# The opening of a fused attention and mixture-of-experts kernel rearranged: who rounds the weights and the context, where the second context half lands, and when batch 0 makes its values

## The reference

```python
x = x + tanh(g_xattn) * attention(layernorm(x), ctx, Wq, Wk, Wv, Wo, bo)   # 8 batches, 512 queries, 1024 keys, 8 heads of 64
x = x + tanh(g_ffn)   * moe(layernorm(x), router, w_pre, w_gate, w_post)   # 8 experts, top 2, capacity, 4096 tokens
```

## Time and profile before

| | us |
|---|---|
| median of 3 runs | 1797.45 |
| lowest, highest | 1796.33, 1798.6 |
| the profiled execution's own time | 1798.76 |
| its span | 1796.9 |

### The profile page before, as it was taken

One profiled execution on the slowest core, in us unless ns is written; L12 is line 12 of the kernel. 1 busy time (PEld: TensorE's weight loads), 2 busy tenths in 40 slices (PEclk: granted clock), 3 DMA queues, 4 the chain that ended last, 5 costly groups with the idle time before them and its releaser, 6 DMA issues. The chain is left out here.

```text
span 1796.9 us, 35848 instructions
## 1 busy us (share of the span) xinstructions
PE 1681.8 (94%) x13198; PEld 1532.6 (85%) x13199; DVE 1270.6 (71%) x2667; ACT 1053.7 (59%) x2229; POOL 678.2 (38%) x619
## 2 busy tenths in 40 slices
PE   5799999999999999999999986599999999999997
PEld 4688888888888888888888875499999999999997
DVE  5688888888888888888988886555555555545443
ACT  3666766666766767667766764244454454545443
POOL 4243344444444444444344323232333333333323
PEclk9999999999999999999999997699999999999999
DMA  6100001010010010010000021432323233231211
GB/s 192 36 10 15 24 25 36 25 36 25 25 36 25 25 36 25 25 36 25 25 25 25 24 71 55 155 101 35 100 37 92 54 75 100 29 104 25 36 30 24
DMA packets 65117, 85.55 MB, mean 48 GB/s; under 512 B 7208, under 2 KB 53800, under 8 KB 65008
## 3 DMA queue, kind: packets, MB, share of 16 engines
q1 hardware_dynamic: 47680, 64.08, 11.3%
q0 software_dynamic: 15984, 18.82, 6.0%
q10 hardware_dynamic: 1344, 1.20, 0.2%
HBM read 54.59 MB, written 29.48 MB: 47 GB/s over the span
## 5 line engine op out<-in xcount | busy, mean ns | idle before, releaser
L699 POOL TENSOR_SCALAR probs<-probs,row_rec 128x1024 f32<-128x1024 f32 x256 | 284.5, 1123 | 490.6 <-DVE row_rec L1525 477.7
L1064 ACT ACTIVATE pt_h<-turned 128x512 fp32r<-128x512 f32 x512 | 279.9, 602 | 218.1 <-PE turned L839 218.0
L1240 DVE TENSOR_TENSOR pt_l<-turned,pt_h 128x512 fp32r<-128x512 f32 x512 | 331.2, 680 | 7.0 <-ACT pt_h L1064 6.0
L1456 DVE TENSOR_REDUCE neg_max<-scores 128x1 f32<-128x1024 f32 x256 | 301.2, 1217 | 38.5 <-PE scores L827 38.5
L839 PE MATMUL turned<-ident,probs 128*128 128x128 f32 x2048 | 282.7, 280 | 30.2 <-DVE pt_l L1240 20.1
L839 PEld LDWEIGHTS turned<-ident,probs 128*128 128x128 f32 x2048 | 224.4, 142 | 98.1 <-issue 66.8
L1113 ACT ACTIVATE probs<-scores,neg_max 128x1024 f32<-128x1024 f32 x256 | 285.2, 1117 | 4.4 <-DVE neg_max L1456 4.3
L943 PE MATMUL ring<-pt_h,v_hl 128*128 128x256 f32 x1024 | 263.7, 295 | 5.5 <-DVE v_hl L1240 5.3
L1692 DVE TENSOR_TENSOR act_f<-ffn,silu 128x256 f32<-128x256 f32 x288 | 122.1, 424 | 195.6 <-ACT silu L1194 190.3
L943 PE MATMUL ring<-pt_l,v_hl 128*128 128x256 f32 x1024 | 253.0, 285 | 0.0
L1194 ACT ACTIVATE silu<-ffn 128x256 f32<-128x256 f32 x288 | 110.6, 384 | 227.4 <-PE ffn L804 216.9
(11 more groups left out here) (221 smaller groups left out, 4060.8 us busy)
## 6 DMA issues: line engine op xcount, KB each, us to landing
w_raw<-w_t SPq DMA_DIRECT2D x16, 1024.0 KB
e_rows<-lists SPq DMA_DIRECT2D x37, 260.0 KB, 2.7
ctx_raw<-ctx_t SPq DMA_DIRECT2D x16, 512.0 KB, 3.8
wg_raw<-wg_t SPq DMA_DIRECT2D x8, 1024.0 KB
lists<-rows SPq DMA_DIRECT2D x8, 520.0 KB, 8.2
x_in<-x SPq DMA_DIRECT2D x8, 512.0 KB, 3.9
x_sum<-x SPq DMA_DIRECT2D x8, 512.0 KB, 3.9
out<-x_sum SPq DMA_DIRECT2D x8, 512.0 KB, 2.9
```

The source lines that it names most:

```text
L699: nc.gpsimd.tensor_scalar(probs[:, k, :], probs[:, k, :], row_rec[:, k:k + 1], 1.0, ALU.mult, ALU.mult).then_inc(scaled, 1)
L1064: return nc.scalar.activation(dst, src, ACT.Copy)
L1240: return nc.vector.tensor_tensor(dst, src, hi_part.bitcast(F32), ALU.subtract)
L1456: nc.vector.tensor_reduce(neg_max[:, k:k + 1], scores[:, n % 2, :].rearrange("p (a c) -> p a c", a=2), AX.XY, ALU.max, negate=True).then_i ...
```

## The change

It touches only what runs before step 9 of batch 0:

- START becomes five jobs in a list of their own, `START_JOBS`: x, x, k, q, k. The four value jobs of batch 0 go into FIRST: two in step 0, one in step 1, one in step 2 (`FIRST_VALUES`).
- ACT rounds the first context half, wk and wq in the order in which they are loaded, then the second context half, and wv after the first k job. Its tanh moves to step 4 of FIRST, behind that step's exponential, and DVE's product of bias and tanh to step 7.
- The second context half is loaded into `probs[:, 2, :]`, right behind wq and without a wait; wk is loaded before wq. The 8 padding writes follow the loads with no wait for the context in front of them.
- DVE makes the lo part of the first context half, between two pieces of the layer norm, and normalises x. POOL keeps the power and makes the lo part of the second context half.
- PE no longer waits for the small inputs at its start, but before step 8 of FIRST.

```diff
+START_JOBS = [("x", 0, 0), ("x", 1, 0), ("k", 0, 0), ("q", 0, 0), ("k", 0, 1)]
+FIRST_VALUES = {0: [("v", 0, 0), ("v", 0, 1)], 1: [("v", 0, 2)], 2: [("v", 0, 3)]}
...
             def start():                                  # SP
                 load_x(0, x_in, x_loaded)
-                load_ctx(0, 0)
-                for i, (w, dst) in enumerate(((wq, probs[:, 0, :]), (wk, probs[:, 1, :]),
...
+                load_first_ctx(0)
+                load_first_raw(0)
+                load_first_raw(1)
+                load_first_ctx(1)
+                load_first_raw(2)
...
-                sp.wait_ge(ctx_split, 1)
-                load_ctx(0, 1)
...
+            power(0, 0)                                   # POOL
+            pool.wait_ge(ctx_hi, 2)
+            nc.gpsimd.tensor_tensor(ctx_l[:, :, M // 2:M], first_ctx_raw(1),
+                                    ctx_h[:, :, M // 2:M].bitcast(F32), ALU.subtract)\
+                .then_inc(ctx_split, 1)
...
-            pe.wait_ge(small_loaded, 64)                  # PE
+            for [(what, c)] in START.steps:
+                run_job(START, NEXT_FROM, what, c)
...
-            act.wait_ge(small_loaded, 64)                 # ACT
-            nc.scalar.activation(tanh_g[:, :], tanh_g[:, :], ACT.Tanh).then_inc(tanh_done, 1)
+                split_first_ctx(0)
+                split_raw(0)
+                split_raw(1)
+                drain(START, NEXT_FROM, *x0)
+                drain(START, NEXT_FROM, *x1)
+                split_first_ctx(1)
+                drain(START, NEXT_FROM, *k0)
+                split_raw(2)
+                drain(START, NEXT_FROM, *q0)
+                drain(START, NEXT_FROM, *k1)
...
+                for part in range(4):                     # DVE
+                    layer(0, 0, x_in, part)
+                v.wait_ge(ctx_hi, 1)
+                lo(ctx_l[:, :, 0:M // 2], ctx_raw[:, :, :], ctx_h[:, :, 0:M // 2])\
+                    .then_inc(ctx_split, 1)
+                for part in range(4, 8):
+                    layer(0, 0, x_in, part)
+                v.wait_ge(ln_ready[0], 1)
+                for q in range(QT):
+                    nc.vector.tensor_scalar(x_in[:, q, :], x_in[:, q, :], norm[:, 0, 4, q:q + 1],
+                                            norm[:, 0, 5, q:q + 1], ALU.mult, ALU.add)\
+                        .then_inc(normed[0], 1)
+                split_first(0)
+                split_first(1)
+                drain(START, NEXT_FROM, *x0)
+                drain(START, NEXT_FROM, *x1)
+                drain(START, NEXT_FROM, *k0)
+                split_first(2)
+                drain(START, NEXT_FROM, *q0)
+                drain(START, NEXT_FROM, *k1)
```

More of the change, by code:

```diff
@@ L113, in __init__ @@
         self.steps, place = [], offset
-        for u in range(UNITS if own or nxt else END_STEPS):
+        for u in range(UNITS if own else END_STEPS if prev else len(START_JOBS)):
             mine = []
+            if not own and not prev:
+                self.steps.append([(START_JOBS[u], place)])
+                place += 1
+                continue
+            if not prev:
+                mine += FIRST_VALUES.get(u, [])
             if u % 4 in (1, 2) and (prev if u < 5 else own):
@@ L130, in __init__ @@
         self.where = {job: c for step in self.steps for job, c in step}
+        self.early = {job: c for step in self.steps[:NEXT_FROM] for job, c in step
+                      if not prev and own and job[:2] == ("v", 0)}
     def results(self, u):
@@ L135, in results @@
             return self.steps[u - 1]
-        return [(job, c - RING) for job, c in self.before.steps[-1]] if self.before else []
+        return [(job, c - RING) for job, c in self.before.steps[-1]] if self.prev else []
     def of(self, b):
@@ L142, in place @@
     def place(self, job):
+        if job in self.early:
+            return self.early[job]
         if SLOT_OF[job] < NEXT_FROM:
@@ L388, in wait_all_drained, with first_raw, whole, first_ctx_raw @@
                     wait_drained(eng, body, max(of_bank))
+        def first_raw(i):
+            flat = x_sum[:, :, :].rearrange("p q d -> p (q d)")
+            return ((wk, wk_h, wk_l, probs[:, 0, :]), (wq, wq_h, wq_l, probs[:, 1, :]),
+                    (wv, wv_h, wv_l, flat))[i]
+        def whole(t):
+            return t[:, :, :].rearrange("p c n -> p (c n)")
+        def first_ctx_raw(half):
+            if half == 0:
+                return ctx_raw[:, :, :]
+            return probs[:, 2, :].rearrange("p (c m) -> p c m", c=KC)
         def batches(eng, run):
-            run(START)
             run(FIRST)
@@ L527, in run @@
                         load_w(sp, i, 0)
+            start()
             batches(sp, run)
@@ L947, in do_job, with run_job @@
                 last.then_inc(filled, 1)
+            def run_job(body, u, what, c):
+                reads = wait_for_job(body, u, what)
+                wait_all_drained(pe, body, reads + [c - 2])
+                do_job(what, ring[:, c % 2, :])
             def run(body):
                 for u, jobs in enumerate(body.steps):
+                    if body is FIRST and u == 8:
+                        pe.wait_ge(small_loaded, 64)
                     if body.own and u % 2 == 0:
@@ L1064, in hi, with split_raw, split_first_ctx @@
                 return nc.scalar.activation(dst, src, ACT.Copy)
[L1066 to L1069 removed]
+            def split_raw(i):
+                _, dst, _, raw = first_raw(i)
+                act.wait_ge(raw_loaded[i], 16)
+                hi(whole(dst), raw).then_inc(raw_hi, 1)
+            def split_first_ctx(half):
+                act.wait_ge(first_ctx[half], 16)
+                hi(ctx_h[:, :, half * (M // 2):(half + 1) * (M // 2)], first_ctx_raw(half))\
+                    .then_inc(ctx_hi, 1)
             def drain(body, u, what, c):
@@ L1143, in run @@
                             hi(w_h[0][i][:, :], w_raw[i][:, :]).then_inc(w_first_hi, 1)
[L1144 to L1150, removed]
+                    if body is FIRST and u == 4:
+                        act.wait_ge(small_loaded, 64)
+                        nc.scalar.activation(tanh_g[:, :], tanh_g[:, :], ACT.Tanh)\
+                            .then_inc(tanh_done, 1)
                     if body is FIRST and u in (5, 9):
@@ L1156, in run, with start @@
                         hi(wo_h[:, part, :], x_sum[:, :, :]).then_inc(raw_hi, 1)
-            act.wait_ge(small_loaded, 64)
-            nc.scalar.activation(tanh_g[:, :], tanh_g[:, :], ACT.Tanh).then_inc(tanh_done, 1)
+            def start():
+                x0, x1, k0, q0, k1 = (step[0] for step in START.steps)
+                split_first_ctx(0)
[8 more added lines that the diff above has]
+                drain(START, NEXT_FROM, *k1)
+            start()
             batches(act, run)
@@ L1492, in run @@
                 for u in range(len(body.steps)):
[L1493 to L1502, removed]
+                    if body is FIRST and u == 7:
                         v.wait_ge(tanh_done, 1)
@@ L1545, in run, with start @@
                                     .then_inc(w_split, 1)
+            def start():
+                x0, x1, k0, q0, k1 = (step[0] for step in START.steps)
+                v.wait_ge(x_loaded, 16)
+                for part in range(4):
[18 more added lines that the diff above has]
+                drain(START, NEXT_FROM, *k1)
             v.wait_ge(consts, CONSTS)
+            start()
             batches(v, run)
```

34 lines of the change are left out of this document (20 added, 14 removed).

## The result

The changed kernel takes 1788.18 us (median of 5 runs, 1787.42 to 1792.13), the kernel before 1797.96 (5 runs, 1796.33 to 1798.62). The ratio is 0.9951, 95% interval 0.994 to 0.9963. The forecast was 1789.9, with a range of 1786.3 to 1794.8.

The account below looks back on a forecast made before the run. PE, busy 1681.8 of 1796.9 us, was taken as the bound, so an earlier start of the common part counts. Terms -8.9 + 1.2 + 0.1 = -7.6 from the median 1797.45 gave 1789.9, range 1786.3 to 1794.8.

Parts of the forecast that it names:

- Term 1: Opening of batch 0: the first scores start at 22.25 instead of 31.16, 8.9 us earlier.
- the wait of `ctx_l` behind the power: Opening: DVE's context split waits for POOL's power until 8.2 and ends at 9.35.
- my sign "longer than 1.21": Opening, new profile: DVE's first `ctx_l` taking longer than 1.21 would show the forecast right.
- my other bound, 8.9: Opening: end of `ctx_l` if the power locks nothing, 8.9; worth -0.5 us.
- the case of `wq_l`: Opening of the kernel before: DVE's `wq_l` took 3.24 against 1.21 for `wk_l`, read as running after POOL's `ctx_l`.
- Term 2: Steps 0 to 4 of batch 0: third pair's row maxima 17.5 after the scores' start, not 16.3; 1.2 us given back.
- Term 3: Small moves: ACT's tanh in step 4 stands ahead of what DVE waits for in step 5; costs 0.1 us.
- Rival 1: Opening: padding writes share engines with loads, wv lands near 25, scores near 28, gain only 2, 1795.5; chance 0.08.
- Rival 3: First steps: TensorE stays at the low clock level, sum +4.2 us, 1801.7; chance 0.05.
- Rival 4: Later in batch 0, DVE's waits in steps 5 and 9: the gain is given back, 1796 to 1799; chance 0.05.
- Rival 2: Opening: clock level rises from the first k job or drains fit better, 2 to 3 us more, 1787.2; chance 0.12.

Follow-up runs that it names:

- experiment 7: Changed kernel with DVE's lo part of each half of wo behind the row maxima of steps 6 and 10; ratio 0.9906 to the kernel before.
- experiment 2: Kernel before with one edit, the value jobs of batch 0 moved from START into steps 0 to 2; ratio 0.9984 to the kernel before.
- experiment 4: Changed kernel with x normalised by GpSimd again; executed once, no time compared, first scores at 24.78.
- experiment 8: The changed kernel again, unaltered, on another chip; ratio 0.995 to the kernel before.
- experiment 1: Changed kernel with the four value jobs of batch 0 back at the end of START, ahead of the first scores; ratio 0.9963 to the kernel before.
- experiment 5: Changed kernel with a second, unused power of 128x4 on GpSimd right behind the first; executed once, no time compared, the second power took 1.41.
- experiment 6: Changed kernel with DVE's lo part of each half of wo moved from steps 5 and 9 to 6 and 10; ratio 0.9896 to the kernel before.

## Why the prediction was right, point by point

- **Term 1, forecast 8.9, measured 31.16 - 21.42 = 9.7.** The step that was off is the wait of `ctx_l` behind the power: I took 9.35 for its end, and it ended at 8.63. 0.3 of that is the context, which ACT rounded from 6.31, not 6.6. The rest is the wait, which isn't there: `ctx_l` took 1.23 beside the power, as any split of this trace (1.22), so my sign "longer than 1.21" shows nothing. In experiment 7 the context came as forecast (rounded from 6.66), and `ctx_l` ended at 8.98, by my other bound, 8.9; the scores started at 22.03 there. I chose wrongly by the case of `wq_l`, in which GpSimd read 1024 columns twice. Here it reads four. The four normalising instructions took 1.38, not 1.1. From x to the scores the schedule held: 11.35 to 22.25 is 10.9, measured 10.85 to 21.42 is 10.6. The later landings, the low level for the first k and most of q, and the drains were as put. What the term consists of was put wrongly. It is not mostly the value jobs, but 5.2 for the earlier first projection (18.90 - 13.72) and 4.6 for the shorter way from there to the scores (12.3 before, 7.7 now), since without the value jobs the low level falls on k and q; experiment 2 gives 4.7 for this part.
- **The rule.** The Trainium skill ("SBUF — State Buffer", section "SBUF: two separate sides") says that, of a VectorE instruction with two SBUF inputs and a GpSimd instruction that reads SBUF, the one that starts first has the shared port pair for its whole length and the other is blocked (the section that the prediction names, "Who interferes with whom", has the contention of the two; the whole length stands here). Two long ones that exclude each other (`wq_l` before, experiment 4) agree with that. The power of 128x4 does not: it started at 7.11 and ran to 8.15, and `ctx_l`, started at 7.40, took its 1.23. Nor does the order of turns in experiment 4, where a split that started at 10.63 went ahead of a GpSimd instruction that had begun at 9.80. Here the measurement decides.
- **Term 2, forecast 1.2, measured 1.3.** The chain of drains and exponentials came as written: second scores 8.6 after the first (8.5), third maxima 17.56 after the first scores (17.5).
- **Term 3, forecast 0.1, measured 0.1.** 47.45 - 38.98 = 8.47 at the third maxima, 8.36 at the copy of x. DVE's product of bias and tanh stayed hidden.
- **Sum.** -9.7 + 1.3 + 0.1 = -8.3 against -7.6. The medians say -9.8, those of experiment 8 -9.6. What is left over, 1.3 to 1.5, is of the size of the spread between executions, and no mark in the trace carries it; where it comes from is open. That the time fell in the range rests on the marks and not on this rest: with the 8.4 alone it would have been 1789.6.
- **Rival 1** (writes beside loads) is refuted: wv took 8.7 from its issue at 3.44 and landed at 12.1, as for a queue served in order (DMA issues after: count, KB, median us from issue to landing; the last small input, issued at 5.58, landed at 13.2):

```profile
x_sum<-wv SPq DMA_DIRECT2D x1, 512.0 KB, 8.7
rw<-rw_t SPq DMA_DIRECT2D x1, 8.0 KB, 7.6
```

- **Rival 3** (TensorE low through the first steps) did not occur, but the low level behind holes is real: experiment 1 shows it (0.77) where the value jobs don't fill them. **Rival 4** is refuted by the marks: nothing is given back. **Rival 2** did not occur either: the first k job ran low (the first matmul in 0.77, above, where the later ones at full clock take 0.39).

## What to carry to other kernels

In a kernel whose later part hangs on one chain, an opening can be summed up instruction by instruction, and what is won there comes out at the end nearly one for one. Jobs that nobody needs yet go into the holes of the first steps; beside the time that they fill, they kept the granted clock up here (1.00 where they stand in the holes, 0.77 and 0.83 where they don't). Two engines that hand over within one step should each have their part where the other's has already ended: moving DVE's part of wo one step on was worth as much as the whole rearranged opening (8.8 and 8.2 at the first store).

## What the runs showed of the hardware that was not expected

- VectorE and GpSimd do not exclude each other whenever a GpSimd instruction runs long: a power of 128x4 (1.04 us) delayed no VectorE split, while two VectorE splits of 1024 columns (1.22 each, back to back) held up a GpSimd instruction of 256 columns until both were done (2.39 for this one instead of 0.55). That it depends on how much is read is my reading; no run varies it alone.
- In experiments 5 and 6 the granted clock fell to 0.83 for one stretch of 10 us in the middle of the attention (400 to 410 and 790 to 800). The first trace of the changed kernel shows none, its repetition, the same kernel, one at 790 to 800. From store to store these batches took 135.4 to 135.5, where the shortest take 131.9. Other batches took 134.0 without a value below 1 in such a stretch, among them the neighbours of the two in experiments 5 and 6. The stage table of experiment 5 around it:

```profile
390.00:400.00 10.00, 8.22 (x58) 6.71 (x58) 9.50 (x17) 5.81 (x12) 5.62 (x4) 1.00 0.30 96
400.00:410.00 10.00, 9.19 (x60) 8.04 (x60) 7.58 (x20) 5.39 (x11) 2.21 (x2) 0.83 0.01 2
```

  PE idled 1.8 of the 10 us ahead of it. I have not found what sets the fall off; it makes single times of this kernel weaker evidence than marks within a trace.
- The clock column of a stage table can read 1.00 where matmuls run low. From 10 to 20 it gives 1.00 for the changed kernel, while of the nine matmuls from 13.72 to 17.27 all but the first start 0.43 apart and take 0.63; from 17.98 on it is 0.23 apart and 0.39. The duration of a matmul is the safer sign.
